# Sixteen-head attention with its query projection in three fp16 passes: the change, the profile before and a prediction

## What is computed

```
xn = layernorm(x)
q  = xn @ Wq                  # 256 -> 16 heads x 128
k  = ctx @ Wk ; v = ctx @ Wv  # 128 -> 8 groups x 128, shared by two heads each
p  = softmax(q k^T / sqrt(128) + mask)
x  = x + (p @ v) @ Wo         # 16 x 128 -> 256
```

## Time and profile before

| | us |
|---|---|
| median of 3 runs | 1300.39 (1295.93 to 1302.8) |
| the profiled execution, its own time | 1297.31 |
| its span, first to last instruction | 1295.6 |
| PE busy / DVE busy / ACT busy / POOL busy | 1146.9 / 992.0 / 860.9 / 317.5 |
| L462 `scores` | 270.3 |
| L766 `p_low` | 260.9 |
| L442 `q_project`, all three layers | 46.4 |
| L449 `qk_project`, all three layers | 26.3 |
| L523 `tail_out`, all three layers | 48.7 |

### The profile page before, as it was taken

How to read it: one execution, slowest core, us unless ns; L and a number is a source line. 1 busy time by engine, 2 the same in 40 slices (tenths; PEclk the granted TensorE clock), 3 DMA queues, 4 the chain that set the end, 5 groups by cost and what they waited for, 6 DMA issues and landing times. The chain is left out here.

```text
span 1295.6 us, 23108 instructions
## 1 busy us (share of the span) xinstructions
PE 1146.9 (89%) x8738; PEld 761.3 (59%) x8742; DVE 992.0 (77%) x1858; ACT 860.9 (66%) x1303; POOL 317.5 (25%) x353
## 2 busy tenths in 40 slices
PE   7999999848776887899899999887998999999987
PEld 3677676635322444486566666645874666666644
DVE  6788878297768883493899989776987998998654
ACT  5777778484454887422877777565976777777563
POOL 3000000100362000000172654502650456275200
PEclk8899999959986999899899999999998999999999
DMA  7999999201374000901899999514745999999600
GB/s 280 172 186 189 188 171 187 84 1 74 82 146 82 2 3 2 245 25 59 162 200 182 206 182 169 130 43 160 205 115 129 180 181 183 178 163 169 123 1 9
DMA packets 450833, 170.00 MB, mean 131 GB/s; under 512 B 437160, under 2 KB 437544, under 8 KB 449064
## 3 DMA queue, kind: packets, MB, share of 16 engines
q1 hardware_dynamic: 450736, 168.72, 62.3%
HBM read 58.84 MB, written 0.26 MB: 46 GB/s over the span
## 5 line engine op out<-in xcount | busy, mean ns | idle before, releaser
L462 PE MATMUL ps<-ctxT,L_xattn_qk 128*128 128x512 f16 x1152 | 270.3, 385 | 0.8 <-DVE L_xattn_mx L742 0.5
L766 DVE SCALAR_TENSOR_TENSOR arena<-L_xattn_sm,L_xattn_rr,arena 128x1024 f16<-128x1024 f32 x192 | 260.9, 1399 | 9.4 <-ACT arena L612 9.4
L597 ACT ACTIVATE L_xattn_sm<-L_xattn_sm,L_xattn_mx 128x2048 f32<-128x2048 f32 x96 | 192.3, 2003 | 75.6 <-DVE L_xattn_mx L742 73.9
L612 ACT ACTIVATE arena<-L_xattn_sm,L_xattn_rr 128x1024 f16<-128x1024 f32 x192 | 210.0, 1140 | 5.2
L462 PEld LDWEIGHTS ps<-ctxT,L_xattn_qk 128*128 128x128 f16 x1152 | 112.5, 99 | 130.1 <-issue 9.9
L484 PE MATMUL ps<-arena,ctx 128*128 128x256 f16 x1488 | 177.7, 273 | 0.0
L484 PEld LDWEIGHTS ps<-arena,ctx 128*128 128x128 f16 x1488 | 145.4, 98 | 31.9
L742 DVE CUSTOM_DVE_ANT_0 L_xattn_sm<-ps,L_xattn_bias 128x1024 f32<-128x1024 f32 x96 | 117.0, 1219 | 55.7 <-issue 55.5
L742 DVE CUSTOM_DVE_ANT_0 L_xattn_sm<-ps,L_xattn_bias,L_xattn_mx 128x1024 f32<-128x1024 f32 x96 | 123.2, 1284 | 2.4 <-DVE L_xattn_mx L742 2.1
L475 PE MATMUL ps<-arena,ctx 128*128 128x128 f16 x1488 | 100.8, 222 | 9.6 <-DMA arena<-arena 9.5
L475 PEld LDWEIGHTS ps<-arena,ctx 128*128 128x128 f16 x1488 | 92.3, 99 | 25.1 <-DMA arena<-arena 13.4
(11 more groups left out here) (585 smaller groups left out, 2082.7 us busy)
## 6 DMA issues: line engine op xcount, KB each, us to landing
L_ffn_ring<-in_L_ffn_experts SPq DMA_DIRECT2D x34, 384.0 KB, 3.6
arena<-in_L_xattn_w SPq DMA_DIRECT2D x36, 320.0 KB, 3.7
arena<-in_L_ffn_experts SPq DMA_DIRECT2D x8, 768.0 KB, 7.7
arena<-in_L_xattn_w SPq DMA_DIRECT2D x6, 640.0 KB, 6.5
arena<-arena SPq DMA_TRANSPOSE x193, 4.5
arena<-in_L_ffn_codes SPq DMA_DIRECT2D x1, 3072.0 KB, 11.2
arena<-in_L_attn_w SPq DMA_DIRECT2D x1, 2163.0 KB, 19.3
arena<-in_L_attn_w SPq DMA_DIRECT2D x2, 1026.0 KB, 5.1
```

The source lines that it names most:

```text
L462: last = nc.tensor.matmul(ps[:, at, :], qk[:, h // 2, qp, h % 2, b * P:(b + 1) * P], k.ctxT[:, cp, b, at * 512:(at + 1) * 512], start=(a = ...
L597: nc.scalar.activation(sm[:, u % 2, :], sm[:, u % 2, :], ACT.Exp, bias=mx[:, u % 2, 1:2], scale=-1.0, accum_out=rs[:, u % 2:u % 2 + 1]).th ...
L612: nc.scalar.mul(pp[:, u % 2, 0, at], sm[:, u % 2, at], rr[:, u % 2:u % 2 + 1]).then_inc(s.p_high, 1)
L766: nc.vector.scalar_tensor_tensor(pp[:, u % 2, 1, at], sm[:, u % 2, at], rr[:, u % 2:u % 2 + 1], pp[:, u % 2, 0, at], ALU.mult, ALU.subtrac ...
```

## The change

The query projection of all three layers is done in three fp16 passes. For this, `xn` transposed is held as a high part (ACT copies it to fp16) and a low part (DVE subtracts it, new line 782), and POOL splits each pair's query weights in two instructions (`split_queries`: a copy to fp16 and a subtraction, 512 columns wide).

In L0 alone, three passes also replace `qk_project` and `tail_out`. POOL's split there is 640 columns wide and takes the key weights in, and `split_out` splits the 512 columns of output weights. DVE makes the low parts of two operands: `query_low` (128x512, PSUM minus SBUF) and `values_low` (128x256). `qk_project` waits for the first, `tail_out` for the second. `tail_values`, and the last half-head's `out_last`, stay in fp32.

POOL reads the query weights some time after they land, so the loads of them are issued earlier: `load_q` of the second pair moves from `u` = 4 to `u` = 0 of the same iteration, and of the first pair from `u` = 0 to `u` = 4 of the iteration before. With this, what each load waits for changes: at `u` = 0 for `qk_psum` of `2i+2` and at `u` = 4 for `2i+3`.

```diff
                         early = first and u < 2
+                        if u == 0 and first:
+                            sp.wait_ge(s.qk_psum, 1)
+                            load_q(1, 0)
                         if u == 0 and not final:
-                            sp.wait_ge(s.qk_psum, 2 * i + 1)
-                            load_q(i + 1, 0)
-                        if u == 4 and not final:
                             sp.wait_ge(s.qk_psum, 2 * i + 2)
                             load_q(i + 1, 1)
+                        if u == 4 and i + 2 <= LASTI:
+                            sp.wait_ge(s.qk_psum, 2 * i + 3)
+                            load_q(i + 2, 0)
...
                     for h in range(2):
                         for c in range(DC):
-                            last = nc.tensor.matmul(PREP[:, h * T:(h + 1) * T], wq[j][:, h, c, :], k.xnT[:, c, :],
-                                                    start=(c == 0), stop=(c == DC - 1))
+                            for a, (wpart, xp) in enumerate(PARTS):
+                                last = nc.tensor.matmul(PREP[:, h * T:(h + 1) * T], wq[j][:, wpart, h, c, :],
+                                                        xh[:, xp, c, :], start=(c == 0 and a == 0),
+                                                        stop=(c == DC - 1 and a == len(PARTS) - 1))
...
                 def qk_project(i, j):
+                    if opening:
+                        pe.wait_ge(s.qT_low, 2 * i + j + 1)
+                        for a, (wpart, qp) in enumerate(PARTS):
+                            last = nc.tensor.matmul(PREP, wqh[:, j, wpart, 512:640], qTh[:, qp, :],
+                                                    start=(a == 0), stop=(a == len(PARTS) - 1))
+                        last.then_inc(s.qk_psum, 1)
+                        return
...
                 def tail_out(i, h):
+                    if opening:
+                        pe.wait_ge(s.oh_low, BODY * i + h + 1)
+                        if h % 2 == 0:
+                            pe.wait_ge(s.wo_low, 2 * i + h // 2 + 1)
+                        for b in range(B):
+                            for part, wpart in PARTS:
+                                last = nc.tensor.matmul(OUT[:, b * D:(b + 1) * D], ohh[:, part, b * P:(b + 1) * P],
+                                                        woh[:, h // 2, wpart, (h % 2) * D:(h % 2 + 1) * D], start=False,
+                                                        stop=True, skip_group_check=True)
+                        last.then_inc(s.out_done, 1)
+                        return
...
+                def split_queries(chain, i, j):
+                    if i == 0 and opening:
+                        pool.wait_ge((g.first_w0, g.first_w1)[j], 16)
+                    elif i == 0:
+                        wait_weights(k, pool, slot, loaded)
+                    else:
+                        pool.wait_ge(wq_sem[j], 16 * i)
+                        pool.wait_ge(s.qT_psum, 2 * i + j - 1)
+                    chain(nc.gpsimd.tensor_copy(wqh[:, j, 0, :], w[:, j, 0:QW]))
+                    nc.gpsimd.tensor_tensor(wqh[:, j, 1, :], w[:, j, 0:QW], wqh[:, j, 0, :], ALU.subtract)\
+                        .then_inc(s.wq_low, 1)
...
                 ln_vector(k, dve, k.x, k.xn, LN_EPS, n)
+                dve.wait_ge(g.xnT_ready, k.xt + 1)
+                nc.vector.tensor_tensor(xh[:, 1, :, :].rearrange("p c t -> p (c t)"), ps[:, 0, :],
+                                        xh[:, 0, :, :].rearrange("p c t -> p (c t)"), ALU.subtract).then_inc(g.xn_low, 1)
```

87 lines of the change are left out of this document (68 added, 19 removed).

## The result

The changed kernel takes 1319.5 us (median of 4, 1317.35 to 1320.35) against 1298.4 us for the kernel before on the same chip: ratio 1.015, 95% interval 1.0123 to 1.0178. The forecast was 1307, with a range up to 1317. The direction was right and the size wrong: +21 us, where the text reckoned +9.5. (The ratio on record, 1.015, lies slightly under the ratio of the two medians, 1.016.)

A forecast was written before the change was run, and what follows sets the result against it. PE was taken to set the pace inside a layer. Starts +14.5, layer norms +0.6, L2 and L3 -5.6, L0 steady 0, loads +2 made +11.5, less 2 for overlap +9.5: 1307 us, range 1296 to 1317.

The forecast's parts named there:

- The starts, the term that decides: Layer starts: the first transpose, behind a load waiting for `qk_project`, comes later; L0 +7.5, L2 and L3 +3.5 us each.
- The 1 us that the forecast put on the clock: Starts of L2 and L3: PE's low clock may last another stretch, so each pays 3.5 us (1.3 to 4.8), shift included.
- until 33.6: Start of L0: `query_low` runs until 33.6, so the first transpose lands at 40.4 to 41 instead of 34.60, +6.2 us.
- Hidden behind `p_high`: Layer starts: POOL's split delays the second `q_project` by 1.5 to 2 us, but this is hidden and costs nothing.
- L0's steady part: L0 after its start: DVE's waits leave a saving of 1.7 us, POOL's collisions cost 2 us, sum about 0.
- POOL's collisions with `p_low`: L0's steady work: POOL's splits slow DVE's `p_low`, costing 0.3 to 0.5 us each period, 2 us over six periods.
- So L2 and L3 save 2.8 us each: Steady work of L2 and L3: `q_project` gets 0.47 us shorter for six pairs, saving 2.8 us in each layer.
- 0.2 us for each layer: Layer starts: the low part of `xn` adds 0.7 us, `q_project` pays back 0.5, leaving 0.2 us; 0.6 in all.
- Loads in steady work: Steady work of the three layers: later loads delay transposes, mostly hidden; 0.7 us a layer, 2 in all (0 to 6).
- Untouched layers: The nine layers whose code is unchanged: the prediction had no term for them, so 0.
- The 2 us taken off for overlap: Whole sum: several small waits overlap, so 2 us were taken off, from +11.5 to +9.5.
- DVE becomes the bound of L0: Rival, L0: POOL's splits hit `p_low` each time, the period grows by 0.8 us, 1313 us in all; chance 0.13.

The follow-up runs named there:

- e1: Changed kernel, with each layer's second load of query weights, in its first iteration, issued behind the first unit's two transposes: 1310.9 us, ratio 1.0079.
- e6: Changed kernel, with POOL's splits for all but the first two pairs of each layer touching one column only: 1317.2 us, ratio 1.0143.
- e7: Changed kernel with three passes for `q_project` alone, query-weight loads one unit later, POOL's first splits in L2 and L3 after `xn`: 1300.1 us, ratio 1.001.
- e5: Changed kernel, with POOL's first split of query weights in L2 and L3 begun only when `xn` is done: 1316.0 us, ratio 1.0159.
- e2: Changed kernel, with the loads of query weights issued one unit later in all iterations, behind the transposes of units 0 and 4: 1308.3 us, ratio 1.007.
- e3: Kernel before, with nothing but the new order of the loads of query weights: 1312.2 us, ratio 1.0094.
- e10: Kernel before, plus one DVE copy of 208 columns without effect ahead of the layer norm of the layer before the last: last layer 57.9 us instead of 55.7.
- e9: Kernel before, plus three DVE copies of 232 columns without effect ahead of the layer norm of the eight-head layer behind L2: 1300.8 us, ratio 1.0016.

## Why the prediction was wrong

By its own steps:

1. **The starts, the term that decides: right in mechanism, 15.1 forecast and 17.5 measured, the layer norms included.** SP's order and its chain came as written, and e1 gives back 8.6 to 11.8 us. In L2 the load behind `qk_project` makes the first product 2.3 us later (forecast 2.5), and without the norm the start costs 2.4 (forecast 3.5); in L3 it is 3.3. The 1 us that the forecast put on the clock did not come in L2: the slowed stretch after its start lasted 10.2 us in two executions and 6.8 in the third (before 6.8, in one 3.4), and L2 stayed within 0.4 us. (Both windows of the earlier trace rows are of L2, so they say nothing of L0.) In L0 the first product comes 8.8 us later where 7.7 were forecast, since `p_low` at 4.95 us delayed `query_low` beyond "until 33.6". "Hidden behind `p_high`" failed here: the second pair's split did not delay its own product but pushed POOL's work on the values onto `p_low`.
2. **L0's steady part: near, by two errors.** The wait at L541 and the period were met within 0.15 us. But the 2 us for POOL's collisions with `p_low` did not come (51 of 51 at their old duration, e6), so six periods kept 1.2 us where the text had 0.
3. **"So L2 and L3 save 2.8 us each": wrong, they save nothing.** L3's six periods are as long as before and L2's 0.4 us longer. This failed step is worth 6.0 us together. Rows 1 had it: DVE was busy for 29.80 of 32 us in L2. I read PE at 31.64 as the only pace, worked out the chain through DVE for L0 and did not for L2 and L3, where DVE has more to do. The idle rows show PE waiting for DVE's `add_mixed`, 0.46 us instead of 0.20, two units after the saving, for ACT's `q_copy` at the other group unit, and in L2 for two late transposes (1.12 and 0.85 us). e7 kept the whole 2.8 us in L0, 1.5 in L3 and none in L2, so it is the layer and not the passes. Which of the three waits would remain if another went was not tried.
4. **"0.2 us for each layer" for the layer norm: wrong, 1.5.** This is 2.6 us in L2 and L3 (e5: 3.3). I looked for POOL's collisions with `p_low` alone, where it was slow in rows 8, and passed over POOL's very first instructions, which start together with the layer norm.
5. **Loads in steady work, 2 us: nothing** (e2, and e3's periods). The late transposes of L2 are counted in step 3.
6. **Untouched layers, 0: on average +5.0.** The text did not price them. Their slowed stretches fall anew with each execution (580.9 to 586.5 with one and the same program) and lay less well in all three executions of the changed kernel. e10 reaches the same lengths in the kernel before by a copy of 0.27 us and by chance.

The 2 us taken off for overlap were wrong, too: the terms added up. From 9.5: +2.4 (1 and 4), -1.2 (2), +6.0 (3), -2.0 (5), +5.0 (6), +2 for the overlap and -0.2 for the rest of the layers make 21.5; the profiles have 16.4 + 5.0 = 21.4. In the first of these terms the norm of step 4 is +2.6 and the rest of the starts -0.2. Of the 11.9 us missed, 5 are the untouched layers and 8.6 the two failed steps, 3 and 4; small errors of the other sign take back the rest.

Of the rivals, "DVE becomes the bound of L0" did not happen; DVE and ACT in part became the bound of L2 and L3, which no rival named.

## What to carry to other kernels

A list that an engine works off in order must be read at its first entries: there a load that waits for a result holds up what the whole machine waits for, while the same load costs nothing once the pipeline is full. A saving on the engine that is busy all the time is worth only what the next engine leaves of it, so follow the chain in each kind of layer and not in the easiest one: with PE at 32.00 and DVE at 27.04 of 32 us the saving of `q_project` came whole (e7, L0), with PE at 31.64 and DVE at 29.80 none of it came (L2). And look at what a newly used engine does in the first microseconds of a layer, beside small instructions on the critical path.

## What the runs showed of the hardware

- A DVE instruction of two columns (L135) took 0.78 us instead of 0.17, and a subtract-and-scale of 256 columns (L139) up to 1.35 us instead of 0.41, beside POOL's copies and subtractions. L135 reads one SBUF tensor, L139 one and two values per partition. Beside POOL's work in L0 and L2 the maxima, which read PSUM and SBUF, kept their 1.22 and 1.28.
- The same program has layers that differ by 2 to 4 us between executions, because stretches at 1.2 GHz fall differently; one execution of the kernel before had none behind L0's first products and was 2.4 us shorter in L0 (234.1). A difference of 5 us in one profile, in layers that were not touched, is not a finding. In the 20 profiles the length of the layer behind L2 follows the distance to L2's slowed stretch: 54.6 us at 207.33 and 207.34 in two different kernels, 52.5 at 207.39.
- A copy of 232 fp32 columns within SBUF on DVE (e9) takes 0.28 us, and three of them 0.57 together, 0.19 from start to start; L139, 256 columns, takes 0.41 and two of them 0.74.
